# Slot attention at the end of a fused network: z times the old slots formed by GpSimd before the last tanh, and the layer norm applied by VectorE, with the steps behind it one round earlier

## The reference

```python
si = slot_input / denom[..., None]
gi = si @ Wih.T + bih ; gh = S @ Whh.T + bhh          # S: the same 64 slots for each batch
r = sigmoid(i_r + h_r); z = sigmoid(i_z + h_z)
n = tanh(i_n + r * h_n)
S_new = (1.0 - z) * n + z * S
q = S_new @ wq + bq ; k = S_new @ wk + bk ; v = S_new @ wv + bv
attn = softmax(q @ k.T * scale)                         # over the slots
y = S_new + attn @ v
y = (y - mean(y)) * rsqrt(var(y) + 1e-05) * ln_g + ln_b
slot_values = y @ wvp + bvp
out = (alpha @ slot_values) @ wo + bo                   # alpha: top-8 routing weights, computed before
x = x + out
```

## Time and profile before

| what | us |
|---|---|
| median of 3 runs | 952.29 (951.01 to 954.82) |
| the profiled execution, its own time | 952.57 |
| span of its profile | 951.3 |
| busy PE, DVE, ACT, POOL over the span | 915.1, 791.6, 794.5, 547.9 |

### The profile page before, as it was taken

How to read it: one execution, slowest core, us unless ns; L and a number is a source line. 1 busy time by engine, 2 the same in 40 slices (tenths; PEclk the granted TensorE clock), 3 DMA queues, 4 the chain that set the end, 5 groups by cost and what they waited for, 6 DMA issues and landing times.

```text
span 951.3 us, 25813 instructions
## 1 busy us (share of the span) xinstructions
PE 915.1 (96%) x8641; PEld 734.2 (77%) x8641; DVE 791.6 (83%) x3563; ACT 794.5 (84%) x2162; POOL 547.9 (58%) x670
## 2 busy tenths in 40 slices
PE   8999999999999999999999999999999999999887
PEld 7899989898989989973325888877777777775566
DVE  6766989989898989989996766768889899896985
ACT  6999989898989988867875999987788888886886
POOL 4444636465564646441795157667788888891041
PEclk9999999999999999999999999999999999999899
DMA  9100000000000000000236899921000000000002
GB/s 375 67 2 2 2 2 2 2 2 2 2 2 2 2 1 2 2 2 0 89 127 196 279 305 303 302 79 29 24 14 24 24 14 24 24 3 2 1 1 89
DMA packets 36226, 57.70 MB, mean 61 GB/s; under 512 B 3456, under 2 KB 27264, under 8 KB 35712
## 3 DMA queue, kind: packets, MB, share of 16 engines
q1 hardware_dynamic: 36096, 56.07, 17.6%
HBM read 40.85 MB, written 11.01 MB: 55 GB/s over the span
## 4 chain that ended last, share of the span: by engine, by line
PE 55%; DVE 18%; ACT 8%; issue 4%; POOL 3%; DVEq 0%; ACTq 0%; POOLq 0%
PE PB L270 5%; PE PB L2151 5%; PE PB L271 4%; PE PB L272 4%; PE PB L437 4%; PE PB L2168 3%; PE PB L390 3%; PE PB L2123 3%; PE PB L459 2%; PE PB L1433 2%; PE PB L1434 2%; PE PB L1435 2%; DVE W L400 2%; ACT W L409 2%; DVE HFXT L607 1%
## 5 line engine op out<-in xcount | busy, mean ns | idle before, releaser
L409 ACT ACTIVATE W<-W,small 128x128 f32<-128x128 f32 x384 | 149.2, 392 | 12.9 <-DVE small L400 12.1
L421 POOL TENSOR_TENSOR W<-W,small 128x512 f32<-128x512 f32 x96 | 100.5, 1052 | 100.3 <-DVE small L415 100.3
L270 PE MATMUL PB<-RR_s 128*128 128x256 f32 (+1 forms) x468 | 151.6, 324 | 5.5 <-DVE RR_s L471 3.8
L271 PE MATMUL PB<-RR_s 128*128 128x256 f32 (+1 forms) x468 | 139.9, 299 | 0.0
L272 PE MATMUL PB<-RR_s 128*128 128x256 f32 (+1 forms) x468 | 139.8, 299 | 0.0
L2139 POOL TENSOR_TENSOR AR_s<-AR_s,small 128x512 f32<-128x512 f32 x128 | 129.7, 1043 | 16.7 <-DVE small L2132 16.7
L2132 DVE CUSTOM_DVE_ANT_0 AR_s<-PB,W 128x128 f32<-128x128 f32 x512 | 111.2, 286 | 2.8 <-PE PB L2123 1.2
L1409 DVE TENSOR_TENSOR RR_s<-AR_s,RR_s 128x512 fp32r<-128x512 f32 (+1 forms) x96 | 66.4, 697 | 42.4 <-ACT RR_s L1402 39.5
L270 PEld LDWEIGHTS PB<-RR_s 128*128 128x128 f32 x468 | 88.8, 190 | 15.6 <-DVE RR_s L471 6.4
L400 DVE CUSTOM_DVE_ANT_0 W<-PB,W 128x128 f32<-128x128 f32 x384 | 86.0, 282 | 13.5 <-PE PB L390 12.8
L349 DVE COPY AR_s<-PB 128x512 f32<-128x512 f32 x128 | 84.7, 682 | 13.2 <-PE PB L272 13.1
(11 more groups left out here) (461 smaller groups left out, 2636.8 us busy)
## 6 DMA issues: line engine op xcount, KB each, us to landing
RR_s<-W1D SPq DMA_DIRECT2D x13, 512.0 KB, 4.4
RR_s<-W2D SPq DMA_DIRECT2D x13, 512.0 KB, 4.8
W<-in_w SPq DMA_DIRECT2D x1, 5895.5 KB, 25.0
RR_s<-XD SPq DMA_DIRECT2D x46, 128.0 KB, 3.0
XD<-RR_s SPq DMA_DIRECT2D x18, 256.0 KB, 3.7
HQ<-W1D SPq DMA_DIRECT2D x6, 512.0 KB, 4.2
HQ<-W2D SPq DMA_DIRECT2D x6, 512.0 KB, 4.9
HQ<-XD SPq DMA_DIRECT2D x22, 128.0 KB, 3.1
```

Of the source, the lines that this page charges most:

```text
L270: nc.tensor.matmul(out, lh, rh, start=True, stop=False)
L271: nc.tensor.matmul(out, ll, rh, start=False, stop=False)
L409: e = nc.scalar.activation(SS[r][:, hl], SS[r][:, hl], ACTF.Exp, bias=mx[r][:, h:h + 1], scale=-1.0, accum_out=rc[r][:, h:h + 1])
L421: nc.gpsimd.tensor_tensor(s3, s3, over(rc[r], 2, [128, 4, 128]), ALU.mult).then_inc(s_nrm, 1)
```

## The change

For step 6 POOL forms z from the z-gate's tanh, as (T2 + 1) * 0.5 into SN by a `tensor_scalar` of 128x512 (L2870 of the new file), and SN times the slots (L2872). At step 7 DVE then forms (T2 - 1) * T3 and adds -0.5 times it to SN (L2821, L2824); the subtraction S - n on POOL is gone. POOL's layer norm part is only eps and pow (L2879, L2881). DVE applies the norm by four `tensor_scalar` of 128x128 with mean and root as columns (L2849), ACT's four are gone, and the transposition of y moves to step 12; every step behind it moves one forward, so that a group has steps 3 to 16. (S_new comes to be the first value of slots_pool + 2, so some wait values change.) Numbers of lines in the new file are a few lower or higher than before.

```diff
@@ -2508,15 +2508,15 @@
                 passes7(("sT", n), la, 13)
             if i == 11:
                 passes7(("pv", n), ld, 19)
+            if i == 12:
+                passes7(("yT", n), la, 14)
             if i == 13:
-                passes7(("yT", n), la, 15)
-            if i == 14:
-                passes7(("vs", n), ld, 28)
+                passes7(("vs", n), ld, 29)
+            if i in (14, 15):
+                passes7(("o", n, i, 0), ld, 30 + 2 * (i - 14))
+                passes7(("o", n, i, 1), ld, 31 + 2 * (i - 14))
             if i in (15, 16):
-                passes7(("o", n, i, 0), ld, 29 + 2 * (i - 15))
-                passes7(("o", n, i, 1), ld, 30 + 2 * (i - 15))
-            if i in (16, 17):
-                passes7(("y", n, i), la, 16 + i - 16)
+                passes7(("y", n, i), la, 15 + i - 15)
...
-            if i == 13:
+            if i == 12:
                 pe_drained7(("yT", n))
-                pe.wait_ge(la, 14)
+                pe.wait_ge(ld, 28)
                 for p in range(4):
                     mm = nc.tensor.transpose(bank7(("yT", n))[:, pairs[p]], T1[:, pairs[p]], ident)
                 mm.then_inc(lp, 1)
...
-            if i in (16, 17):
-                c = 2 * n + i - 16
+            if i in (15, 16):
+                c = 2 * n + i - 15
                 pe_drained7(("y", n, i))
-                pe.wait_ge(ld, 30 + 2 * (i - 16))
+                pe.wait_ge(ld, 31 + 2 * (i - 15))
...
@@ -2779,17 +2779,11 @@
                 act.wait_ge(lp, 12)
                 nc.scalar.activation(T1, bank7(("sT", n))[:, :], ACTF.Copy).then_inc(la, 1)
             if i == 12:
-                act.wait_ge(ld, 19)
-                act.wait_ge(s_ll[n], 6)
-                for p in range(4):
-                    t = nc.scalar.activation(T1[:, pairs[p]], T1[:, pairs[p]], ACTF.Identity, bias=dn7[:, p:p + 1], scale=rs7[:, p:p + 1])
-                t.then_inc(la, 1)
-            if i == 13:
                 act.wait_ge(lp, 14)
                 nc.scalar.activation(T2, bank7(("yT", n))[:, :], ACTF.Identity, bias=w("flnb"), scale=w("flng")).then_inc(la, 1)
...
@@ -2824,9 +2818,10 @@
             if i == 7:
                 dve.wait_ge(la, 4)
                 dve.wait_ge(s_ll[n], 1)
-                nc.vector.scalar_tensor_tensor(SN, T2, 1.0, SN, ALU.add, ALU.mult).then_inc(ld, 1)
+                nc.vector.scalar_tensor_tensor(T2, T2, 1.0, T3, ALU.subtract, ALU.mult).then_inc(ld, 1)
+                dve.wait_ge(s_ll[n], 2)
                 dve.wait_ge(ld, 9)
-                nc.vector.scalar_tensor_tensor(SN, SN, 0.5, T3, ALU.mult, ALU.add).then_inc(ld, 1)
+                nc.vector.scalar_tensor_tensor(SN, T2, -0.5, SN, ALU.mult, ALU.add).then_inc(ld, 1)
...
-            if i == 14:
+            if i == 12:
+                dve.wait_ge(s_ll[n], 5)
+                for p in range(4):
+                    t = nc.vector.tensor_scalar(T1[:, pairs[p]], T1[:, pairs[p]], mv7[:, 2 * p:2 * p + 1], rs7[:, p:p + 1],
+                                                ALU.subtract, ALU.mult)
+                t.then_inc(ld, 1)
+            if i == 13:
...
         def pool_slots(n, i):
             T2, T3, SN, VV, VS = tiles[n]
             dn7, mx7, sm7, rs7, bn7, mv7 = stats[n]
-            if i == 7:
-                pool.wait_ge(s_la[n], 4)
-                nc.gpsimd.tensor_tensor(v8(SN), slot8, v8(T3), ALU.subtract).then_inc(s_ll[n], 1)
+            if i == 6:
+                pool.wait_ge(s_la[n], 3)
+                nc.gpsimd.tensor_scalar(SN, T2, 1.0, 0.5, ALU.add, ALU.mult).then_inc(s_ll[n], 1)
+                pool.wait_ge(s_ll[n], 1)
+                nc.gpsimd.tensor_tensor(v8(SN), v8(SN), slot8, ALU.mult).then_inc(s_ll[n], 1)
             if i == 8:
                 pool.wait_ge(s_ld[n], 10)
                 nc.gpsimd.tensor_tensor(VS, SN, w("fbv").broadcast_to([128, 512]), ALU.add).then_inc(s_ll[n], 1)
             if i == 11:
+                m7 = mv7.rearrange("p (q s) -> p q s", s=2)
                 pool.wait_ge(s_ld[n], 27)
-                m7 = mv7.rearrange("p (q s) -> p q s", s=2)
                 nc.gpsimd.tensor_scalar(rs7.unsqueeze(2), m7[:, :, 1:2], 1e-5, None, ALU.add).then_inc(s_ll[n], 1)
-                nc.gpsimd.tensor_scalar(dn7.unsqueeze(2), m7[:, :, 0:1], -1.0, None, ALU.mult).then_inc(s_ll[n], 1)
-                pool.wait_ge(s_ll[n], 3)
+                pool.wait_ge(s_ll[n], 4)
                 nc.gpsimd.tensor_tensor(rs7, rs7, mhalf, ALU.pow).then_inc(s_ll[n], 1)
-                pool.wait_ge(s_ll[n], 5)
-                nc.gpsimd.tensor_tensor(dn7, dn7, rs7, ALU.mult).then_inc(s_ll[n], 1)
```

More of the change, by code:

```diff
@@ L2701, in pe_slots @@
                 pe_drained7(("sT", n))
-                pe.wait_ge(s_ll[n], 2)
+                pe.wait_ge(s_ll[n], 3)
                 for p in range(4):
@@ L2717, in pe_slots @@
                 mm.then_inc(lp, 1)
-            if i == 14:
+            if i == 13:
                 pe_drained7(("vs", n))
                 pe.wait_ge(s_s7a, 1)
-                pe.wait_ge(la, 15)
+                pe.wait_ge(la, 14)
                 for p in range(4):
@@ L2724, in pe_slots @@
                 mm.then_inc(lp, 1)
-            if i in (15, 16):
-                c = 2 * n + i - 15
+            if i in (14, 15):
+                c = 2 * n + i - 14
                 outs = [bank7(("o", n, i, hh)) for hh in range(2)]
@@ L2730, in pe_slots @@
                 pe.wait_ge(s_att, c + 1)
-                pe.wait_ge(ld, 28)
+                pe.wait_ge(ld, 29)
                 for p in range(2):
@@ L2781, in act_slots @@
             if i == 12:
-                act.wait_ge(ld, 19)
-                act.wait_ge(s_ll[n], 6)
-                for p in range(4):
-                    t = nc.scalar.activation(T1[:, pairs[p]], T1[:, pairs[p]], ACTF.Identity, bias=dn7[:, p:p + 1], scale=rs7[:, p:p + 1])
-                t.then_inc(la, 1)
-            if i == 13:
                 act.wait_ge(lp, 14)
                 nc.scalar.activation(T2, bank7(("yT", n))[:, :], ACTF.Identity, bias=w("flnb"), scale=w("flng")).then_inc(la, 1)
-            if i in (16, 17):
-                c = 2 * n + i - 16
-                act.wait_ge(lp, 18 + i - 16)
+            if i in (15, 16):
+                c = 2 * n + i - 15
+                act.wait_ge(lp, 18 + i - 15)
                 nc.scalar.activation(cs(XT, c), bank7(("y", n, i))[:, :], ACTF.Copy).then_inc(la, 1)
@@ L2854, in dve_slots @@
                 nc.vector.tensor_tensor(v4(VS), v4(bank7(("vs", n))[:, :]), over(bvo, 1, [128, 4, 128]), ALU.add).then_inc(ld, 1)
-            if i in (15, 16):
-                c = 2 * n + i - 15
+            if i in (14, 15):
+                c = 2 * n + i - 14
                 x4 = cs(XF, c).rearrange("p (q hh t) -> p q hh t", q=2, hh=2)
-                dve.wait_ge(lp, 16 + i - 15)
+                dve.wait_ge(lp, 16 + i - 14)
                 for hh in range(2):
@@ L3097, in sp_attend2 @@
             for c in range(CH):
-                sp.wait_ge(s_la[c // 2], 16 + c % 2)
+                sp.wait_ge(s_la[c // 2], 15 + c % 2)
                 nc.sync.dma_start(out_d[4 * c:4 * c + 4, :, :].rearrange("b t d -> t b d"), v4(cs(XT, c))).then_inc(s_out, 16)
```

2 lines of the change are left out of this document (1 added, 1 removed).

## The result

The changed kernel takes 960.7 us (median, 958.31 to 962.52); the kernel before took 951.92 us in the same comparison (950.26 to 954.82). The ratio is 1.0092, 95% interval 1.0080 to 1.0103: 8.8 us slower. The profiled execution has a span of 959.3 us. The forecast was 959.9 us: the sum came out, its terms did not all.

A forecast was written before the change was run, and what follows sets the result against it. The prediction saw three successive bounds: the POOL chain, ACT's rounds, PE's tail. Its terms +2.45, +6.2 and -1.0 gave +7.65 us, added to 952.29 for a forecast of 959.9 us, range 954.5 to 962.

The forecast's parts named there:

- Stretch one: Up to the sum y of group 0: GpSimd's new SBUF reads hold up VectorE, +2.45 us.
- the walk: Step through GpSimd's and VectorE's queues before group 0's sum y, whoever starts first holding SBUF: +2.45 us.
- The gain without any contention: Before group 0's sum y: removing S - n from GpSimd saves 1.5 us if nothing else happened.
- Stretch two: From the sum y of group 0 to that of group 3: 19.4 us instead of 13.17, +6.2 us.
- The ring: Between sums y: statistics, pow, VectorE's norm, PE's transposition and next L2710 form a loop, 6.1 us per round against 4.4.
- VectorE's norm: Four tensor_scalar of 128x128 per group between pow and PE's transposition: 0.65 us, 0.95 at most.
- v's bias behind the first pow: On GpSimd, group 3's bias starts before VectorE's norm of group 0 and makes it wait: +0.9 us.
- Stretch three: From the sum y of group 3 to the end: its transposition comes sooner, -1.0 us.
- 9.75 us, no change: PE's tail, from group 3's transposition to the last eviction: same pieces in the same order, still 9.75 us.
- The ring alone: Rival: GpSimd's instructions fall into gaps and hold up nobody, +2.8 us, 955.1 us; chance 0.15.
- Not slower: Rival: ACT's relief counts and the loop between sums y doesn't close, 948.3 or 949.8 us; chance 0.15.
- Slow scalar: Rival: GpSimd's tensor_scalar for z takes 1.65 us, +9.5 us in all, 961.8 us; chance 0.1.

The follow-up runs named there:

- e8: The changed kernel with GpSimd's scalar and product of step 6 replaced by memsets, which read no SBUF: 961.76 us, ratio 1.0095 to the kernel before.
- e9: e8 with six filler matmuls ahead of PE's wait for the norm: 956.86 us, ratio 1.0053 to the kernel before.
- e10: e4 with GpSimd's v bias of group 3 moved ahead of its root steps of group 0: 957.27 us, ratio 1.0057 to the kernel before.
- e5: Kernel before, with VectorE applying the norm after GpSimd's two root steps, slots part and everything behind the norm at their old steps: 953.2 us, ratio 1.0017.
- e6: Kernel before, with the norm left on ScalarE and only what stands behind it issued a round sooner: 965.47 us, ratio 1.0134.
- e4: The changed kernel with six filler matmuls of 128x128 ahead of PE's wait for the norm: 957.5 us, ratio 1.0072 to the kernel before.
- e2: The changed kernel with the slots part undone, so only the norm part and its sooner steps remain: 959.71 us, ratio 1.0093 to the kernel before.

## Why the prediction was right, and where its terms were off

**Stretch one, +2.45 forecast, +0.38 measured.** The mechanism was right and the sizes too large. GpSimd's scalar, for which I took L421's 1.04 us, took 0.62, near the lower bound of 0.525; the product 1.10 instead of 1.28. So both were through at 897.78, and L2612 took 0.46 us instead of 0.43: its +0.6 did not come. L2821 and L2824 of the first group cost 0.44 and 0.70 us, 1.1 instead of 2.3. Later GpSimd made L2824 0.22 us longer (0.76 in the walk) and L2814 0.42 and 0.88 (0.85 and 1.1). Who came first hung on little: the walk has GpSimd's scalar 0.16 us ahead of L2821, the trace 0.03 (902.31 against 902.34). The gain without any contention, which I put at 1.5 us, is 23.71 - 22.25 = 1.46 in e8 and e9. The Trainium skill, "SBUF — State Buffer", section Who interferes with whom, states that a VectorE instruction with two SBUF inputs contends with a GpSimd instruction that reads SBUF, and not with one that only writes it. The trace agrees: with the reads gone (e8) L2821 and L2824 took 0.68 and 0.69 us. The norm (L2849) is another case, since it reads one SBUF tensor and two columns; the runs show only that it took 1.83 us beside GpSimd's v's bias and 1.11 with the bias moved (e10), not which ports it used.

**Stretch two, +6.2 forecast, +8.22 measured.** The ring is what the prediction said, by PE's queue and VectorE's queue; e5 and e6 show that it hangs on the sooner step. The term that was mis-sized is VectorE's norm: I had 0.65 us for four, from L568's 0.416 us for 512 elements, and they take 1.11. A bare round is 6.45 us (e4) against the 6.1 of the working; 0.46 of norm explains it, less some 0.1 that other links were shorter. v's bias behind the first pow cost 0.72 us instead of 0.9; it did start first (922.86 against the norm's 922.92)., which the prediction cites for that, leave out the short multiplication between pow and the bias. The rest, 1.3 us, is a term that the sum put at nothing: PE's lower clock behind its new waits.

**Stretch three, -1.0 forecast, +0.66 measured.** At full clock (e2, e4) it is 13.61 against 14.35: -0.74, so the step was nearly right. In the profiled execution of the changed kernel the same missing term cost 1.4 us. "9.75 us, no change" for PE's tail was the wrong step: it was 11.14 us (945.81 to 956.95) at a clock of 0.86. With the clock at 1.00 (e4, 943.77 to 953.52) it is 9.75 us, so only the clock was missing from it.

**The sum** was right by luck in its sizes, because the errors have both signs: 2.1 us too much in stretch one, and in the others too little: 1.0 for the ring and the last norm, 2.7 for the clock. Of the profiled spans that makes +9.3 where +7.65 was forecast; the medians have +8.8.

**The rivals.** "The ring alone" (955.1) was too low because GpSimd's work does hold up VectorE and because the ring is longer. "Not slower" fell with the first PE wait of 1.63 us. "Slow scalar" was the opposite of what happened.

**Open.** Why the clock fell behind some of PE's waits and not behind others isn't settled. It did not fall behind the 1.81 us at 939.01, nor in e2 behind three waits of 2.29 us, the same length as the last of the changed kernel, behind which it did. The fillers show that with PE busy in these waits it stayed at 1.00. The loss may also differ between executions: the fastest of the six of the changed kernel (958.31 us) has a mean granted clock of 0.995 over its whole span, the others (960.13 to 962.52 us) 0.991 to 0.993. The mean is of the whole span, so it doesn't show where the difference lies; the 2.7 us are those of the profiled execution alone. Fillers in the router phase ahead of this one weren't tried; between 860 and 893 the clock is 0.90 in all twelve profiles.

## What to carry to other kernels

When a step is moved sooner, look in the queue of the engine that waits for it, not at the engine that does it: here PE's transposition, put ahead of the next group's matmuls, turned four independent groups into a ring, and in e6 it did so without a norm in VectorE's queue. The same norm at the old step cost 1.6 us, at the new one 8.9. And where a new wait makes PE idle, add to the price what its clock may lose behind it: 2.7 us in the execution profiled here, and none in the one with six useless matmuls ahead of each wait.

## What was not expected of the hardware

- A GpSimd `tensor_scalar` with two constants takes 0.62 us for 128x512 fp32, where a multiplication by a repeated column takes 1.04. Where a VectorE instruction with two SBUF tensors had started 0.1 to 0.2 us before it, it took 1.00 and 1.05 us (after, 908.43 and 912.83).
- A VectorE `tensor_scalar` with two scalars per partition, in place, 128x128 fp32, takes 0.34 us for one and 1.11 us for four in a row; L568's 0.416 us for 512 elements gave 0.65 for four, which was too little.
- The lower clock, 1.2 GHz: L2710's eight matmuls take 1.06 us at 925.36 and 1.91 us at 931.95, behind a wait of PE of 2.61 us; with filler matmuls ahead of the waits they took 1.06 us in all three rounds (e4).
